# Mixture-of-experts tail: six read-back loads go from ScalarE's queue to SyncE's, and the sums over experts are spread differently over the last twelve jobs

## What is computed

```python
h = _layernorm(x, axis=-1) * (1 + cb) + sb
x = x + gb * _L0_ffn_ref(h, ...)
# inside _L0_ffn_ref, for each of the 4096 tokens:
probs = softmax(x @ w_router.T)            # 8 experts
vals, idx = top_k(probs, 2)                # two experts for a token
acc = gelu(x @ Ws1.T + bs1) @ Ws2.T + bs2  # the shared expert, every token
acc = acc + sum over the two of gate * (gelu(x @ W1[e].T + b1[e]) @ W2[e].T + b2[e])
return SCALE * acc
```

## Time and profile before

| what | us |
|---|---|
| median of three runs | 533.95 |
| the three runs | 533.95, 541.45, 533.62 |
| the profiled execution: its own time | 533.95 |
| the profiled execution: its span | 532.1 |

### The profile page before, as it was taken

The page is one execution under the profiler, slowest core; times in us unless marked ns, Lnnn a source line. Parts: engine busy times, 40 slices in busy tenths (PEclk is TensorE's granted clock), DMA queues, the critical chain, the costliest instruction groups (busy, mean ns, idle before and its releaser), DMA issues.

```text
span 532.1 us, 13354 instructions
## 1 busy us (share of the span) xinstructions
PE 489.5 (92%) x4030; PEld 445.3 (84%) x4030; DVE 383.9 (72%) x1613; ACT 363.9 (68%) x1383; POOL 345.7 (65%) x521
## 2 busy tenths in 40 slices
PE   3699999999999999999899889799999989999881
PEld 3389999999999999999647778779999978899881
DVE  4688889888898888898678875426676445353577
ACT  3369999899999989999759569545444544555450
POOL 4257667676777676775220888888888887757740
PEclk9999999999999999999998989899999999999996
DMA  9999800000000000000000114535447678987977
GB/s 197 341 401 393 335 3 2 2 2 2 2 2 2 2 2 2 2 2 2 1 2 0 43 42 135 190 96 155 146 145 212 197 218 264 284 270 226 386 226 215
DMA packets 39277, 68.51 MB, mean 129 GB/s; under 512 B 7474, under 2 KB 25780, under 8 KB 39204
## 3 DMA queue, kind: packets, MB, share of 16 engines
q1 hardware_dynamic: 30900, 53.54, 32.5%
q0 software_dynamic: 4320, 8.99, 4.7%
q10 hardware_dynamic: 3984, 5.12, 2.9%
HBM read 38.16 MB, written 29.46 MB: 127 GB/s over the span
## 4 chain that ended last, share of the span: by engine, by line
PE 79%; issue 5%; DMA 4%; ACT 4%; DVE 4%; SPq 3%; another core or an unknown queue 1%; POOLq 0%; POOL 0%; ACTq 0%; DVEq 0%
PE bank L1418 35%; PE bank L663 13%; PE bank L677 12%; PE bank L636 3%; PE bank L619 2%; DMA xt<-xs 2%; DMA xr<-in_L_attn_x_dram 1%; PE bank L645 1%; PE bank L569 1%; PE bank L558 1%; PE bank L594 1%; SPq L216 1%; ACT hs L786 1%; PE bank L567 1%; DMA yg<-ys 1%
## 5 line engine op out<-in xcount | busy, mean ns | idle before, releaser
L1295 POOL DMA_INDIRECT ys<-yo,dst x71 | 69.2, 974 | 36.1 <-issue 15.7
L1287 POOL DMA_INDIRECT xs<-hrow,slot_i x64 | 62.3, 974 | 38.0 <-issue 38.0
L797 ACT ACTIVATE hid<-bank,slab 128x256 f32<-128x256 f32 (+1 forms) x172 | 62.2, 446 | 26.6 <-PE bank L663 15.8
L677 PE MATMUL bank<-slab,hid 128*128 128x128 f32 x568 | 70.8, 276 | 0.7 <-issue 0.7
L677 PEld LDWEIGHTS bank<-slab,hid 128*128 128x128 f32 x568 | 69.2, 192 | 2.4 <-issue 0.9
L663 PE MATMUL bank<-hg,slab 128*128 128x256 f32 (+1 forms) x344 | 69.0, 344 | 2.0 <-issue 1.7
L1174 DVE TENSOR_TENSOR yb<-bank,slab 128x256 f32<-128x256 f32 (+1 forms) x43 | 16.3, 378 | 62.8 <-PE bank L677 35.9
L663 PEld LDWEIGHTS bank<-hg,slab 128*128 128x128 f32 x344 | 55.0, 191 | 7.2 <-issue 2.8
L805 ACT COPY hg<-bank 128x256 f32<-128x256 f32 (+1 forms) x43 | 14.5, 340 | 51.4 <-PE bank L645 26.8
L1276 POOL MEMSET rested<- 128x1408 f32 x32 | 41.3, 1292 | 0.0
L2311 POOL TENSOR_TENSOR nH<-aH,ones 128x128 f32<-128x128 f32 x32 | 14.6, 455 | 33.8 <-ACT aH L1767 33.8
(11 more groups left out here) (423 smaller groups left out, 1803.8 us busy)
## 6 DMA issues: line engine op xcount, KB each, us to landing
slab<-in_slabs_dram SPq DMA_DIRECT2D x43, 578.0 KB
xs<-fill SPq DMA_DIRECT2D x34, 528.0 KB, 7.4
xt<-xs SPq DMA_DIRECT2D x28, 132.0 KB
yg<-ys ACTq DMA_DIRECT2D x7, 512.0 KB, 5.1
out_dram<-xr SPq DMA_DIRECT2D x18, 64.0 KB
ys<-yo,dst POOLq DMA_INDIRECT x71
xr<-in_L_attn_x_dram SPq DMA_DIRECT2D x4, 256.0 KB, 6.5
xs<-hrow,slot_i POOLq DMA_INDIRECT x64
```

The source lines that it names most:

```text
L677: mm = pe.matmul(y[:, s * D:(s + 1) * D], hid[i % 2][:, n, s * P:(s + 1) * P], right, start=(n == 0), stop=(n == FT - 1), skip_group_check ...
L797: nc.scalar.activation(hid[i % 2][:, n, 0:w], e_half(i, n)[:, 0:w], ACT.Gelu_apprx_tanh, bias=bias).then_inc(e_x, 1)
L1287: pool.indirect_dma_start(out=xs[:, :], out_offset=bass.IndirectOffsetOnAxis(ap=slot_i[:, i, c:c + 1], axis=0), in_=hrow[:, c, :], in_offs ...
L1295: pool.indirect_dma_start(out=ys[:, :], out_offset=bass.IndirectOffsetOnAxis(ap=dst[v][:, s:s + 1], axis=0), in_=yo[v][:, s, :], in_offset ...
```

## The change

The loads 0 to 5 are issued by SyncE in place of ScalarE. `LOAD_AT` is 37. In the SP loop, behind `weights(37)`, stand the ten waits for the first 31 tiles and `load(0)`; `load(1)` to `load(3)` stand behind `weights(38)`, `weights(39)` and `weights(40)`. After the loop, ahead of `store(0)`, stand the ten waits for the first 36 tiles and `load(4)`, `load(5)`. The group steps are spread anew: steps 0 to 5 are behind jobs 38 to 40, two to each, 6 to 11 behind jobs 41 to 46, one to each, 12 to 15 behind job 47 and 16 behind job 48.

```diff
+LOAD_AT = BY_HALF + 6
@@ tail_sync
                 if j >= N_FULL + 2:
                     weights(j)
+                if j == LOAD_AT:
+                    scattered(sp, BY_HALF)
+                if LOAD_AT <= j < LOAD_AT + 4:
+                    load(sp, j - LOAD_AT)
+            scattered(sp, BY_THREE)
+            load(sp, 4)
+            load(sp, 5)
             store(sp, 0)
             store(sp, 2)
             scattered(sp, N_TILES)
@@ tail_scalar
             for i in range(len(JOBS)):
                 e_high(i + 1)
                 e_gelu(i)
-                if i == len(JOBS) - 11:
-                    scattered(act, BY_HALF)
-                    for g in range(4):
-                        load(act, g)
-                elif i == len(JOBS) - 3:
-                    scattered(act, BY_THREE)
-                    load(act, 4)
-                    load(act, 5)
@@ tail_vector
-            SUMS = {-10: (0, 1), -9: (2,), -8: (3,), -7: (4,), -6: (5,), -5: (6,), -4: (7,), -3: (8, 9, 10, 11), -2: (12, 13, 14, 15, 16)}
+            SUMS = {-12: (0, 1), -11: (2, 3), -10: (4, 5), -9: (6,), -8: (7,), -7: (8,), -6: (9,), -5: (10,), -4: (11,), -3: (12, 13, 14, 15), -2: (16,)}
```

## The result

The change makes the kernel slower by a little: the ratio to before is 1.0061, with a 95% interval of 1.0033 to 1.0091 (medians 538.65 and 535.77 us over 20 runs each). The ratios in this document compare only executions in the chip's usual state and leave out the few slow ones, so they differ a little from a quotient of medians. 533.4 against 533.95 had been forecast.

What follows compares the result with a forecast made beforehand. TensorE, busy 92% of the span, was taken as the bound, so only its late idle time and the end could change: 533.95 + 0.6 - 1.1 = 533.4 us, with an 8-in-10 range from 530.4 to 536.0.

Steps and rivals of the forecast that it cites:

- Part 5: TensorE up to job 47: it waits for the last slab, tile 42's, and job 47 starts 0.6 us later.
- Part 4: VectorE behind job 38: stands 3 us for load 0; delay 2.4 us at most, 0.5 us from job 41 on.
- Part 6: The end: fewer group steps left behind job 47 and load 6 issued earlier, a gain of 1.1 us.
- Part 1: ScalarE's queue: six load issues, 2.8 us, go; gain taken as 0.
- Part 2: Load start times: load 0 at about 490.9, loads staggered over 12 us; the 1.46 us tile wait should go.
- Part 3: SyncE's queue: each load costs about 0.5 us; tile 38's rows and slab 0.9 us later.
- The rule of the Trainium skill that I weighed: SyncE's ring: a tile load behind a 512 KB load waits 1.2 us; hitting one on the path gives 534.6.
- C: Slower rival: VectorE's wait for load 0 decides, SyncE never catches up, job 47 +2.3 us; 535.5, chance 0.21.
- A: The forecast itself: the two effects nearly cancel; 533.4 (532.5 to 534.5), chance 0.46.
- B: Faster rival: full DMA engines were the whole trouble, staggering returns 2.3 us and the end 1.1; 530.5, chance 0.23.
- D: No-effect rival: loads 1 to 3 start later, steps wait, VectorE ends with as much left; 533.9, chance 0.10.

Runs made afterwards that it cites:

- r3: Changed kernel with loads 0 to 3 spread behind gelu 39 to 42 and loads 4, 5 behind gelu 44, all on ScalarE; new group steps kept: ratio to before 1.0082.
- r4: Kernel before with loads 0 to 3 spread on ScalarE behind gelu 39 to 42, loads 4 and 5 behind gelu 44, old group steps: ratio to before 1.0041.
- r2: Changed kernel with the group steps put back as before, loads still on SyncE: ratio to before 1.0042.
- r7: Changed kernel with the group steps one job later, step 0 behind job 39: ratio to before 0.9995.
- s2: r7 again, in a later group beside the changed kernel: ratio to before 1.0014.
- r1: The changed kernel again with no edit: ratio to before 1.0075.
- n3: Changed kernel with group steps one job later and load 7 on SyncE behind load 6: ratio to before 0.9986.
- s4: n3 with group step 11 left behind job 47: ratio to before 0.9969.
- n4: Kernel before, burst of four loads kept, with loads 4 and 5 early, load 7 on SyncE behind load 6, group steps respread: ratio to before 0.9989.
- r5: Kernel before, loads in a burst on ScalarE as before, with the changed kernel's group steps: ratio to before 1.0027.
- n1: The changed kernel again with no edit, in a later group: ratio to before 1.0052.
- s1: The changed kernel again with no edit, in the last group: ratio to before 1.0068.
- r8: Changed kernel with load 7 on SyncE right behind load 6 in place of ScalarE: ratio to before 0.9998.
- s3: r8 again, in a later group beside the changed kernel: ratio to before 1.002.
- r6: Kernel before with only loads 4 and 5 earlier, on ScalarE behind gelu 44 and not gelu 47: ratio to before 0.9996.

## Why the prediction was wrong

The kernel got slower where a gain of 0.5 us was forecast, and two terms of the sum failed. Part 5 gave TensorE +0.6 us, because Part 4 let VectorE's delay heal and saw no other way on to TensorE; job 47's add came 1.6 us late. Part 6 gave the end -1.1 us, because it let load 6 land as before; the end cost 1.2 us more. In the first profile the second is the larger miss.

**Part 1** (ScalarE without the loads, 0) fits: r3 and r4 leave the loads there and are no better than after and r2.

**Part 2** (when the loads start): right about load 0, at 487.13 or 2.05 after job 37's add (forecast 490.9, or 1.95). The 3.8 us that it wanted to win back were read too high: they count 1.0 us for a group of matmuls, which TensorE's own timeline shows at its usual length, at 506.10. The waits were 2.8 us.

```profile
506.10 1.06 PE L663 MATMUL bank<-hg,slab 128*128 128x128 f32 x8
```

Its conclusion that the tile load of 6.75 us would go was right, and the one that TensorE's wait would go with it was wrong: the wait moved one tile on and grew to 2.50, and the DMA engines were full again (share 1.02 from 497.10 on).

**Part 3** (what SP pays) charged 0.9 us to the slab of tile 38. It went out at 4.3 after job 37's add, before at 4.4: a wait absorbed the load's issue.

**Part 4** (VectorE's wait) was close in each number: 3 us forecast and 3.27 measured, job 39's add 1.3 late (1.6), job 40's 2.4 (2.7), job 41's 0.5 (0.7). What it said of the outcome, that the delay stays at 0.5 us from job 41 on, is the first step that failed: it was 0.7 until job 43, and 1.4 from job 44 on. I followed the delay down VectorE's own queue, where it does heal, and not through SyncE's: `weights(39)` waits for job 39's add, and the rows of tile 40 stand behind it in the queue.

**Part 5** sized this by the slab of tile 42 alone and took +0.6 us. That slab was in fact only 0.8 us late in its issue (503.50 - 485.08 = 18.4, before 17.7), less than the 1.4 I gave it. TensorE had been stopped before it, by tile rows. Job 47's add came 1.6 us late in the first profile and 3.2 in the mean of four against the mean of two of before (30.6 against 27.4).

**Part 6** took -1.1 us for the end, and has the wrong sign. VectorE was freed as worked out. But I let load 6 start 0.4 us earlier and land in 4.17 us as before. The wait for the last scatter binds it: 4.67 us behind job 47's add against 4.21. And before, SyncE issued load 6 at 520.19 and ScalarE load 7 at 520.56, since each had its stores first; now both queues are free and wait for one semaphore, both loads start within 0.02 us, and load 6 lands 1.4 us later. From load 6's issue to the last step it is 9.84 against 9.07. Together +1.2 us where -1.1 stood. The second step that failed is thus the term "4.17 us for load 6", taken from a row whose conditions the change removed, with the earlier start of load 6 beside it.

The rule of the Trainium skill that I weighed, one ring for the tile rows and the loads, was not the harm where I looked for it (r3 has two rings and the same wait), and its other half, two rings sharing, fits the harm at the end, where I did not look. What I gave as the trace's agreement, that ScalarE's 2.1 MB were still in their ring as the tile load got through, is shown only in part: by the earlier trace rows some 1.3 MB had been moved at most by 494.82, so 0.8 MB were left when the tile load was issued (an estimate), but no row of before shows when the last of it landed.

**Rivals.** C named the right direction and the place where the trouble starts, VectorE's wait for load 0. It had 0.21. Its 535.5, +1.6 us, lies a little under what the ratio gives (+1.8 to +4.9), and its path was right only in part. I made its condition a late landing of load 0 (6 us or more), and VectorE went on 5.1 us after the issue; job 47 started 1.6 us late and not 2.3; SyncE's last slab was nearly on time; and the end cost 1.2 us where C let it give 0.7. The forecast A is refuted, B too (r4). D, that nothing would be gained because the steps wait, is not what happened. The chance for a change within 2% holds.

**Open.** r2 and r4 measured 0.4% slow although VectorE doesn't wait; the end explains 0.75 us or 0.14% of that. In the later groups the same spread of the loads, there with the steps spread too (r7, s2), shows 0.9995 and 1.0014. r2 and r4 weren't run again in a later group, so whether spread loads cost more under the conditions of the first stays open, and with it some 0.3% of the 0.75% that r1 showed there.

## What to carry over

A wait put into an in-order queue costs what stands behind it in every queue that it releases: follow the delayed instruction through all of them, not only down its own. Before taking a transfer's duration from a row, ask who else will start at that moment once the change is made. And consumers can be spread only as early as the landing of their load allows: one job later (r7, s2) the same spreading was free, and with the two loads in one ring as well it came out level with before or slightly ahead (n3 0.9986, s4 0.9969).

## What the runs showed of the hardware

**A scatter beside a group step.** The indirect write on GpSimd takes 0.96 us, but 1.36 to 1.48 when a group step of 0.69 us has started 0.04 to 0.16 us before it; 1.28 at 0.24, 1.15 at 0.38, 1.02 at 0.50, and 0.96 from 0.56 on, or where the step starts after the scatter. In all eighteen profiles these fit one line: the scatter ends no sooner than 1.52 us from the start of the step that it found running, 0.83 us from its end. Three scatters that started within 0.03 us of the step (n4 0.00, r3 0.02, r5 0.03) took 0.96 or 0.97, as if they had come first. POOL in the changed kernel, then in s4, where step 12 had started at 508.19:

```profile
515.11 1.41 POOL L1295 DMA_INDIRECT ys<-yo,dst  x1 [1.64 <-DVE yo L1179]
```

```profile
508.43 1.28 POOL L1295 DMA_INDIRECT ys<-yo,dst  x1 [1.66 <-DVE yo L1179]
```

Before, a step had started 0.56 us ahead of the last scatter, just early enough not to lengthen it. In the changed kernel it is 0.12 us, which is the 0.45 us more ahead of load 6. So in s4 the step was exchanged and not the overlap; 508.19 + 1.52 = 509.71 is where its scatter ends.

The Trainium skill, "SBUF — State Buffer", section "SBUF: two separate sides", says that VectorE with two inputs in SBUF and GpSimd reading SBUF lock each other out for a whole instruction, whoever came first. The group steps have two such inputs, and the trace agrees in one direction, that a scatter which comes second waits. In the other it doesn't: the step that started 0.05 us after the last scatter of before took its usual 0.68 us. That it is this lock, no run shows.

**A memset beside a gate.** A memset of `rested` on GpSimd takes 1.29 us, and the gate of a half tile on VectorE (L1179, some 0.3 us else) that meets it ends only 0.07 to 0.09 us after it, in each of the more than twenty such meetings in sixteen profiles. Here r1, after job 41's add:

```profile
504.91 1.95 DVE L1179 TENSOR_SCALAR yo<-yb,gt 128x128 f32<-128x128 f32 x1
```

```profile
505.49 1.29 POOL L1276 MEMSET rested<- 128x1408 f32 x1
```

The first profile of the changed kernel has little of this (its gate takes 0.72 us): job 42's add follows job 41's by 1.87 us there and by 2.62 in r1, n1, s1, r8 and s3. So up to 0.75 us of the difference between profiles comes from here, and no run takes it apart from the wait for load 0.

**TensorE's clock after the waits.** In three of the four profiles of the changed kernel (r1, n1, s1), and in r5, r6 and n4, the granted clock fell behind the waits for tile rows; in neither of before. A wait alone doesn't decide it: r2, r4 and r8 waited 2.7 to 3.0 us there, and their clock stayed at 1.00. Two windows of s1 (columns as in the earlier trace rows), and TensorE there:

```profile
502.70:506.70 4.00, 2.09 (x15) 1.90 (x15) 3.71 (x20) 1.23 (x5) 2.06 (x4) 0.88 1.03 377
506.70:510.70 4.00, 4.00 (x27) 4.00 (x27) 1.84 (x9) 2.04 (x7) 1.79 (x2) 0.69 0.99 346
```

```profile
506.46 1.91 PE L685 MATMUL bank<-slab,hid 128*128 128x128 f32 x8
```

At 0.69 the mean lies between the two levels, 2.4 and 1.2 GHz, and the eight matmuls of a half tile take 1.91 us where they take 1.06 at the upper one. So s1 lost some 0.12 x 4 + 0.31 x 4 = 1.7 us on top of the waits (an estimate from the two windows). This is a part of why the changed kernel's stretches reach 49.7 us.

**Load 1** took 8.39 us from issue to landing in s1, by its chain, and VectorE waited for it a second time:

```profile
488.14 8.39 DMA yg<-ys
```

```profile
496.56 0.69 DVE L1127 TENSOR_TENSOR ysum<-yg 128x512 f32<-128x512 f32 x1 [2.71 <-DMA yg<-ys]
```

The 4.2 to 5.1 us of the earlier trace rows are those of loads 6 and 7 at the very end; the first four aren't in that view. In n2, the kernel before again, load 0 landed 4.1 us after its issue and the three behind it after 6.0 to 9.6.
